# A recurrent step of 36 single-column products: joint gate banks, an earlier cell tanh, `h2` by halves and a new order of products

## What is computed

```python
xi = xt @ U_i + b_i;  xg = xt @ U_c + b_c;  xo = xt @ U_o + b_o     # all steps
def step(h, c):
    i = sigmoid(xi_t + h @ V_i)
    g = tanh(xg_t + h @ V_c)
    o = sigmoid(xo_t + h @ V_o)
    c_new = h * c + i * g          # the factor of c is h; the f gate is not used
    h_new = o * tanh(c_new)
```

## Time and profile before

| | us |
|---|---|
| Median of 3 runs | 21443.61 (21435.93 to 21449.04) |
| The profiled execution, its own time | 21427.66 |
| Its span (first to last instruction) | 21425.9 |
| TensorE, products busy | 14188.0 (66%) |
| TensorE, weight loads busy (beside the products) | 10794.4 (50%) |
| VectorE busy | 11134.5 (52%) |
| ScalarE busy | 7413.2 (35%) |
| GpSimd busy | 6033.6 (28%) |

### The profile page before, as it was taken

The page is one execution under the profiler, slowest core; times in us unless marked ns, Lnnn a source line. Parts: engine busy times, 40 slices in busy tenths (PEclk is TensorE's granted clock), DMA queues, the critical chain, the costliest instruction groups (busy, mean ns, idle before and its releaser), DMA issues. The chain is left out here.

```text
span 21425.9 us, 696512 instructions
## 1 busy us (share of the span) xinstructions
PE 14188.0 (66%) x249848; PEld 10794.4 (50%) x249849; DVE 11134.5 (52%) x57848; ACT 7413.2 (35%) x56381; POOL 6033.6 (28%) x6537
## 2 busy tenths in 40 slices
PE   5416778822883565665777777777777777777776
PEld 3211236621452444444566666666666666666665
DVE  6325666641125545445455555555555555555555
ACT  0007841100110020010255555555555555555554
POOL 1676666675705747657100000000000000000000
PEclk9858987756996777777755555555555555555555
DMA  0000012301003333333100000000000000000000
GB/s 29 16 5 5 1 39 82 81 12 48 23 25 98 103 75 102 89 88 102 32 4 4 4 4 4 4 4 4 4 4 4 4 4 4 4 4 4 4 4 15
DMA packets 344107, 610.30 MB, mean 28 GB/s; under 512 B 152419, under 2 KB 222154, under 8 KB 340328
## 3 DMA queue, kind: packets, MB, share of 16 engines
q0 software_dynamic: 251520, 473.04, 8.8%
q1 hardware_dynamic: 89704, 98.43, 1.4%
HBM read 506.71 MB, written 64.29 MB: 27 GB/s over the span
## 5 line engine op out<-in xcount | busy, mean ns | idle before, releaser
L2024 PE MATMUL lr_Z<-ls_h,ls_V 128*128 128x1 f16 x225000 | 7182.9, 166 | 2968.8 <-DVE ls_h L2072 2828.3
L2024 PEld LDWEIGHTS lr_Z<-ls_h,ls_V 128*128 128x128 f16 x225000 | 6670.4, 105 | 3969.6 <-DVE ls_h L2072 3825.8
L2066 DVE SCALAR_TENSOR_TENSOR ls_c<-ls_S,ls_hc 128x1 f32<-128x1 f32 x12500 | 2371.0, 219 | 3616.6 <-ACT ls_S L2042 3616.6
L2041 ACT ACTIVATE ls_S<-lr_Z 128x1 f32<-128x1 f32 x12500 | 2068.8, 171 | 5248.9 <-PE lr_Z L2024 5248.9
L1985 POOL COPY ls_HT<-ls_h 128x250 f32 x50 | 19.8, 395 | 10760.5 <-DVE ls_h L2074 10760.5
L620 PE MATMUL prop_sum<-prop_G,prop_S 128*128 128x256 f32 x5040 | 1903.9, 557 | 1668.5 <-DMA prop_G<-hop_table,prop_idx 1267.3
L607 POOL DMA_INDIRECT prop_G<-hop_table,prop_idx x2520 | 2388.0, 948 | 1353.1 <-issue 807.2
L620 PEld LDWEIGHTS prop_sum<-prop_G,prop_S 128*128 128x128 f32 x5040 | 1432.1, 292 | 2140.2 <-issue 955.0
L2072 DVE TENSOR_TENSOR ls_h<-ls_S,ls_th 128x1 f16<-128x1 f32 x12500 | 1892.1, 162 | 800.6 <-ACT ls_th L2049 9.9
L2049 ACT ACTIVATE ls_th<-ls_c 128x1 f32<-128x1 f32 x12500 | 2095.6, 198 | 0.0
L2046 ACT ACTIVATE ls_S<-lr_Z 128x1 f32<-128x1 f32 x12500 | 2068.7, 171 | 0.0
(11 more groups left out here) (407 smaller groups left out, 14492.9 us busy)
## 6 DMA issues: line engine op xcount, KB each, us to landing
prop_G<-hop_table,prop_idx POOLq DMA_INDIRECT x2520
hop_table<-gnn_H SPq DMA_DIRECT2D x3, 6400.0 KB, 20.3
me_W<-in_L_ffn_W SPq DMA_DIRECT2D x16, 1024.0 KB, 10.8
moe_out<-me_Ys SPq DMA_DIRECT2D x108, 128.0 KB, 1.7
gm_AG<-gat_atable,gm_idx POOLq DMA_INDIRECT x840
gs_G<-gat_table,gs_idx POOLq DMA_INDIRECT x840
sd_records<-sc_ring_recsd,sc_ring_placesd POOLq DMA_INDIRECT x784, 2.1
ss_records<-me_ring_recss,me_ring_placess POOLq DMA_INDIRECT x432, 2.1
```

The source lines that it names most:

```text
L2024: mm = nc.tensor.matmul(Z[hf][bank][:, col:col + 1], (V2 if part == "21" else V1)[:, q, ROWS.index(row), :], hx[:, prev, q:q + 1], start=F ...
L2041: nc.scalar.activation(S[:, s % 2, m:m + 1], Z[hf][m][:, col:col + 1], ACT.Sigmoid, scale=back)
L2066: nc.vector.scalar_tensor_tensor(c[:, e, m:m + 1], S[:, e, KD + m:KD + m + 1], S[:, e, m:m + 1], hc[:, m:m + 1], ALU.mult, ALU.add).then_i ...
```

## The change

1. `PLACE` puts i0 and i1 into bank 0, g0 alone into bank 1, g1 alone into bank 2, and o0 and o1 into bank 3.
2. `ORDER` is a list written out product by product. The first 18 finish g0 (at the 15th) and i0 and i1 (at the 18th), products 19 to 24 finish g1, and 25 to 36 both output rows. The first product that reads the second half of `h1` is the fifth; the first to read `h2` of the first half is the twelfth, of the second half the fifteenth.
3. TensorE waits once per step for each of the four semaphores (`h1_made[0]`, `h1_made[1]`, `h2_made[0]`, `h2_made[1]`), in front of the first product that needs it.
4. ScalarE has six instructions a step: tanh of g0, sigmoid of both i, tanh of g1, tanh of the first half of the cell, sigmoid of both o, tanh of the second half of the cell. Each has its own wait.
5. VectorE computes `h2` in two halves directly from its sources, h2 = tanh(c) * o - h1 (with o as a per-partition scalar operand), behind both halves of `h1`; `h` and `hc` come after it. The first cell update waits for g0 and both i, the second for g1; the first half of `h1` waits for the output gates, the second for the second tanh.
6. `h1` and `h2` keep two steps rather than 250.

```diff
-PLACE = {"i0": (0, 0), "g0": (0, 1), "i1": (1, 0), "g1": (1, 1), "o0": (2, 0), "o1": (3, 0)}
+PLACE = {"i0": (0, 0), "i1": (0, 1), "g0": (1, 0), "g1": (2, 0), "o0": (3, 0), "o1": (3, 1)}
...
-ORDER = (terms("i0 g0 i1 g1", "11 21", 0) + terms("i0 g0 i1", "11 21", 1)
-         + [t for q in range(KD) for t in terms("i0 g0", "12", q)]
-         + terms("g1", "11 21", 1) + [t for q in range(KD) for t in terms("i1 g1", "12", q)]
-         + [t for row in ("o0", "o1") for q in range(KD) for t in terms(row, "11 21 12", q)])
+ORDER = terms("g0.21.0 i0.21.0 i1.11.0 i0.11.0 i1.11.1 i0.21.1 g0.11.0 i0.11.1 g0.21.1 g0.11.1 i1.21.0 "
+              "i0.12.0 i1.12.0 g0.12.0 g0.12.1 i0.12.1 i1.21.1 i1.12.1 "
+              "g1.11.0 g1.12.0 g1.11.1 g1.21.1 g1.12.1 g1.21.0 "
+              "o1.21.1 o1.11.1 o0.21.0 o0.11.0 o1.11.0 o0.12.0 o0.12.1 o1.12.1 o0.21.1 o1.21.0 o1.12.0 o0.11.1")
...
-        h1 = ph.sb("h1", [P, BODY, KD], F16)
-        h2 = ph.sb("h2", [P, BODY, KD], F16)
+        h1 = ph.sb("h1", [P, 2, KD], F16)
+        h2 = ph.sb("h2", [P, 2, KD], F16)
...
-                                hx, made = (h2, h2_made) if part == "12" else (h1, h1_made[q])
-                                if (part == "12", q) not in waited:
-
+                                hx, made = (h2, h2_made[q]) if part == "12" else (h1, h1_made[q])
+                                if made not in waited:
                                     pe.wait_ge(made, i * BODY + s + 1)
                                     waited.append(made)
...
-                            for m in range(KD):
-                                act.wait_ge(z[m], t + 1)
-                                nc.scalar.activation(S[:, s % 2, m:m + 1], Z[hf][m][:, col:col + 1], ACT.Sigmoid, scale=back)
-                                nc.scalar.activation(S[:, s % 2, KD + m:KD + m + 1], Z[hf][m][:, col + 1:col + 2], ACT.Tanh,
-                                                     scale=back).then_inc(gates[m], 1)
-                            for m in range(KD):
-                                act.wait_ge(z[2 + m], t + 1)
-                                nc.scalar.activation(S[:, s % 2, 2 * KD + m:2 * KD + m + 1], Z[hf][2 + m][:, col:col + 1], ACT.Sigmoid, scale=back)
-                            for m in range(KD):
-                                act.wait_ge(cell[m], t + 1)
-                                nc.scalar.activation(th[:, s % 2, m:m + 1], c[:, s % 2, m:m + 1], ACT.Tanh).then_inc(tanh_made[m], 1)
+                            act.wait_ge(z[1], t + 1)
+                            nc.scalar.activation(S[:, e, KD:KD + 1], Z[hf][1][:, col:col + 1], ACT.Tanh, scale=back)
+                            act.wait_ge(z[0], t + 1)
+                            nc.scalar.activation(S[:, e, 0:KD], Z[hf][0][:, col:col + KD], ACT.Sigmoid, scale=back).then_inc(i_made, 1)
+                            act.wait_ge(z[2], t + 1)
+                            nc.scalar.activation(S[:, e, KD + 1:KD + 2], Z[hf][2][:, col:col + 1], ACT.Tanh, scale=back).then_inc(g_made, 1)
+                            act.wait_ge(cell[0], t + 1)
+                            nc.scalar.activation(th[:, e, 0:1], c[:, e, 0:1], ACT.Tanh)
+                            act.wait_ge(z[3], t + 1)
+                            nc.scalar.activation(S[:, e, 2 * KD:M6], Z[hf][3][:, col:col + KD], ACT.Sigmoid, scale=back).then_inc(o_made, 1)
+                            act.wait_ge(cell[1], t + 1)
+                            nc.scalar.activation(th[:, e, 1:2], c[:, e, 1:2], ACT.Tanh).then_inc(th1_made, 1)
...
-                                dve.wait_ge(tanh_made[m], t + 1)
-                                nc.vector.tensor_tensor(h1[:, s, m:m + 1], S[:, e, 2 * KD + m:2 * KD + m + 1], th[:, e, m:m + 1],
+                                dve.wait_ge(o_made if m == 0 else th1_made, t + 1)
+                                nc.vector.tensor_tensor(h1[:, e, m:m + 1], S[:, e, 2 * KD + m:2 * KD + m + 1], th[:, e, m:m + 1],
                                                         ALU.mult).then_inc(h1_made[m], 1)
+                            for m in range(KD):
+                                dve.wait_ge(h1_made[m], t + 2)
+                                nc.vector.scalar_tensor_tensor(h2[:, e, m:m + 1], th[:, e, m:m + 1], S[:, e, 2 * KD + m:2 * KD + m + 1],
+                                                               h1[:, e, m:m + 1], ALU.mult, ALU.subtract).then_inc(h2_made[m], 1)
                             nc.vector.tensor_tensor(h[:, s, :], S[:, e, 2 * KD:M6], th[:, e, :], ALU.mult).then_inc(h_made, 1)
                             dve.wait_ge(h_made, t + 1)
-                            nc.vector.tensor_tensor(h2[:, s, :], h[:, s, :], h1[:, s, :], ALU.subtract).then_inc(h2_made, 1)
                             nc.vector.tensor_tensor(hc[:], h[:, s, :], c[:, e, :], ALU.mult).then_inc(hc_made, 1)
```

More of the change, by code:

```diff
@@ L1812, with terms @@
 ROWS = [g + str(m) for g in GATES for m in range(KD)]
-PLACE = {"i0": (0, 0), "g0": (0, 1), "i1": (1, 0), "g1": (1, 1), "o0": (2, 0), "o1": (3, 0)}
+PLACE = {"i0": (0, 0), "i1": (0, 1), "g0": (1, 0), "g1": (2, 0), "o0": (3, 0), "o1": (3, 1)}
 BANKS = 4
-def terms(rows, parts, q):
-    return [(row, part, q) for row in rows.split() for part in parts.split()]
-ORDER = (terms("i0 g0 i1 g1", "11 21", 0) + terms("i0 g0 i1", "11 21", 1)
-         + [t for q in range(KD) for t in terms("i0 g0", "12", q)]
-         + terms("g1", "11 21", 1) + [t for q in range(KD) for t in terms("i1 g1", "12", q)]
-         + [t for row in ("o0", "o1") for q in range(KD) for t in terms(row, "11 21 12", q)])
+def terms(text):
+    return [(row, part, int(q)) for row, part, q in (t.split(".") for t in text.split())]
+ORDER = terms("g0.21.0 i0.21.0 i1.11.0 i0.11.0 i1.11.1 i0.21.1 g0.11.0 i0.11.1 g0.21.1 g0.11.1 i1.21.0 "
+              "i0.12.0 i1.12.0 g0.12.0 g0.12.1 i0.12.1 i1.21.1 i1.12.1 "
+              "g1.11.0 g1.12.0 g1.11.1 g1.21.1 g1.12.1 g1.21.0 "
+              "o1.21.1 o1.11.1 o0.21.0 o0.11.0 o1.11.0 o0.12.0 o0.12.1 o1.12.1 o0.21.1 o1.21.0 o1.12.0 o0.11.1")
 assert len(ORDER) == len(set(ORDER)) == 3 * KD * M6
@@ L1975, in lstm_layer @@
             z = [pr.sem(f"z{g}") for g in range(BANKS)]
-            gates, cell, tanh_made, h1_made = ([pr.sem(f"{n}{j}") for j in range(KD)] for n in ("gates", "cell", "tanh", "h1_"))
-            h_made, h2_made, hc_made, kept = (pr.sem(n) for n in ("h", "h2", "hc", "kept"))
+            cell, h1_made, h2_made = ([pr.sem(f"{n}{j}") for j in range(KD)] for n in ("cell", "h1_", "h2_"))
+            i_made, g_made, o_made, th1_made, h_made, hc_made, kept = (pr.sem(n) for n in ("i", "g", "o", "th1", "h", "hc", "kept"))
             with pr.block() as block:
@@ L2012, in _ @@
                         for s in range(BODY):
-                            hf, prev = s // HALF, (s - 1) % BODY
+                            hf, prev = s // HALF, (s - 1) % 2
                             waited = []
@@ L2054, in _ @@
                     for m in range(KD):
-                        nc.vector.memset(h1[:, BODY - 1, m:m + 1], 0.0).then_inc(h1_made[m], 1)
-                    nc.vector.memset(h2[:, BODY - 1, :], 0.0).then_inc(h2_made, 1)
+                        nc.vector.memset(h1[:, 1, m:m + 1], 0.0).then_inc(h1_made[m], 1)
+                        nc.vector.memset(h2[:, 1, m:m + 1], 0.0).then_inc(h2_made[m], 1)
                     nc.vector.memset(hc[:], 0.0).then_inc(hc_made, 1)
@@ L2061, in _ @@
                             for m in range(KD):
-                                dve.wait_ge(gates[m], t + 1)
                                 if m == 0:
                                     dve.wait_ge(hc_made, t + 1)
-                                nc.vector.scalar_tensor_tensor(c[:, e, m:m + 1], S[:, e, KD + m:KD + m + 1], S[:, e, m:m + 1], hc[:, m:m + 1],
-                                                               ALU.mult, ALU.add).then_inc(cell[m], 1)
+                                    dve.wait_ge(i_made, t + 1)
+                                else:
+                                    dve.wait_ge(g_made, t + 1)
+                                nc.vector.scalar_tensor_tensor(c[:, e, m:m + 1], S[:, e, KD + m:KD + m + 1], S[:, e, m:m + 1],
+                                                               hc[:, m:m + 1], ALU.mult, ALU.add).then_inc(cell[m], 1)
                             if s % HALF == 0:
```

2 lines of the change are left out of this document (1 added, 1 removed).

## The result

| | before | after |
|---|---|---|
| Median, us | 21444.75 (4 runs) | 21701.06 (4 runs, 21695.46 to 21705.34) |
| The profiled execution, its own time | 21427.66 | 21703.19 |
| Ratio after/before, 95% interval | | 1.012 (1.0102 to 1.0137) |
| Length of most steps, us | 1.700 | 1.733 |
| Steps over 0.2 us longer than that, turns left out | 0 | 200 |

The changed kernel is 256 us slower. The forecast was 21250, faster. The step was to be 1.669 us and is 1.733; and there is a second loss, steps that are 0.23 or 0.34 longer than the others, of which the forecast knew nothing. A turn is the jump from one body of 250 steps to the next.)

A forecast was written before the change was run, and what follows sets the result against it. The prediction took latency round the ring of one recurrent step, 1.700 us, as the bound. Its terms summed to 1.669 a step, 6250 x 0.031 = 194 us saved, giving 21250 us; the range for 8 in 10 was 21040 to 21445.

The forecast's parts named there:

- gate to cell: From the joint input sigmoid's start to the first cell update: 0.205 us instead of 0.266, saving 0.061 a step.
- Products: TensorE's 36 products a step: count and pace of 0.027 us stay, so fewer waits bring zero.
- rival 4: TensorE's pace moves with the waits gone, or the clock goes to 2.4 GHz: about 1.44 a step, 19,800 us; chance 0.02.
- The wait at product 15: TensorE's fifteenth load waits for the second half of `h2`: 0.009 us a step.
- Tanh to `h1`: First cell tanh to first `h1`, output sigmoid now behind the tanh: gap 0.101, sigmoid 0.167, in all 0.301 instead of 0.226.
- Rival 1: On ScalarE the output sigmoid goes 0.067 behind the first cell tanh: step 1.636, 400 us less, 21044; chance 0.12.
- Rival 3: On ScalarE the output sigmoid waits for the whole first tanh, 0.203: step 1.771, 444 us more, 21888; chance 0.09.
- `h2` per half: On VectorE the second half of `h2` starts 0.135 us behind the first, making the fifteenth product 0.009 late.
- Rival 2: On VectorE the halves of `h2` are 0.16 apart, the second 0.037 late: step 1.697, 19 us less, 21425; chance 0.12.
- `h` and `hc`: On VectorE, moved behind both halves of `h2`: `hc` ends 0.59 after the load, hidden with 0.30 to spare.
- The sum: Whole step: 1.669 us against 1.700; 6250 x 0.031 = 194 us saved, forecast median 21250.
- The second half of `h1`: Comes 0.093 us behind the first half, the second tanh waiting for the output sigmoid; hidden with 0.019 to spare.

The follow-up runs named there:

- Experiments 1 and 2: First: changed kernel, gates' wait put before the `hc` wait, 21268.98 us, ratio 0.9921; second: kernel before, `hc` wait put before the gates' wait, 21723.11 us, ratio 1.0132.
- experiment 1: Changed kernel with the wait for the input gates put before the wait for `hc` at the first cell update; 21268.98 us, ratio 0.9921 to before.
- experiment 5, e10: e1_swap with VectorE's semaphores raised by one before the loop and all its waits at t + 2; 22927.01 us on a slower chip, ratio 0.9908 to before.
- experiment 6: Five edits to e1_swap, each alone: output sigmoid first, `h2` in one instruction behind `h`, single sigmoids, old product order, wait every load; steps 1.686, 1.721, 1.714, 1.784, 1.667.
- experiment 6, fifth: e1_swap with a wait in front of every one of the 36 weight loads, as before; step 1.667, 23044 us against 23141 for before.
- e1_swap: Changed kernel with the gates' wait before the `hc` wait at the first cell update; 21268.98 us, ratio 0.9921 to before, step 1.667.
- e12: e10 run again on the chip of e11; 21213.21 us against 21420.23 for before, ratio 0.9904.
- e11: e1_swap run again, on one chip with e12; 21255.17 us against 21420.23 for before, ratio 0.9922.
- e2: Kernel before with the `hc` wait moved ahead of the gates' wait at the first cell update; 21723.11 us, ratio 1.0132 to before.
- e5: Changed kernel with a third wait, for `hc` once more, behind the two at the first cell update; step 1.720, 23379 us against 23141 for before.

## Why the prediction was wrong, point by point

**The step that failed: gate to cell.** "Now i is last, one instruction ..., so 0.172 + 0.033 = 0.205" took the 0.033 from a wait that the update carries itself. It does in the kernel before, where the gates' wait stands first. The diff puts it second, and the update then carries the wait for `hc`: 0.274. That is 0.069 too little there, against 0.005 too much in the other parts together: 0.064 a step, 400 us of the 469 between the forecast of the profiled run, 21234, and that run. Experiments 1 and 2 show it from both sides. The row was there to be read: the trace of before has a semaphore instruction on L2064 in every step and none on L2062. I had listed the added waits, but asked of none which instruction carries it and what is behind it. The rivals didn't have it either: the slower one put the loss on ScalarE, between tanh and sigmoid, where there was none.

**What was missing: the long steps.** 57 us of the 469; 10 more come from ahead of the recurrence. They fall on the edges of the blocks of 128. That an edge costs something where VectorE's stream isn't issued ahead is an inference, from where the eight places are and what removed them: it isn't issued ahead where a wait stands outside of an instruction and is met late (in front of the cell update) or where the value of the waits is replaced (in front of `h2`). Each of the two has its four places in a body, and each went with its own edit: the first four with experiment 1, the others with experiment 5 or 6. The forecast said of the turns alone that issue takes time, and the sum had no term for it elsewhere.

**Right, or nearly:**
- *Products.* Zero for the waits: experiment 6, fifth. The pace is 0.0267 a load and the clock half, as before: rival 4 is out. The wait at product 15 was to be 0.009 and is about 0.012 (its load goes 0.388 after the first, the pace alone gives 0.376); first load to sigmoid 0.696 against 0.692.
- *Tanh to `h1`.* The gap behind the tanh is 0.109, I took 0.101; the sigmoid behind it takes 0.153, I took 0.167; in sum 0.295 against 0.301. Rival 1, a gap of 0.067, is out. The figure of the Trainium skill (ScalarE: Activation LUTs, "What ACT_TABLE_LOAD costs", an overlap of about 93 ns) gave 0.110 for the gap; the trace agrees, 0.203 - 0.109 = 0.094. Rival 3, beside which the prediction named the Trainium skill's rule (Advanced Engine Details and Errata, "The Read-Write Bubble"), isn't seen: by their rows the two overlap by those 0.094.
- *`h2` per half.* The two are 0.136 apart, from 4.008 to 4.144 in the changed kernel; taken 0.135. Rival 2 is out.
- *`h` and `hc`.* `hc` ends at 4.62, 0.60 after the load; taken 0.59. Hidden.
- *The sum.* With the waits in the other order it holds: 1.669 was said, 1.667 is measured; 21250 was said, 21269 and 21255 are measured. The 19 us between forecast and e1_swap are 35 of long steps, which the sum didn't have, less 12 for the shorter step.
- *The second half of `h1`.* 0.091 behind the first half in the changed kernel, taken 0.093. In e1_swap, whose step I had meant, it is 0.101, since the second tanh waits for its cell: the near tie fell the other way, and product 5 still doesn't wait (its load goes at 0.110, the pace alone gives 0.109).

**What stays open.** What VectorE's issue side does in the 0.036 before the semaphore instruction and the 0.045 behind it. Why the third wait saves 0.013. Why the step of e12 is 1.663 where e10's, the same kernel, is 1.667: the fifth load goes at 0.105 rather than 0.109, but in e11 it goes at 0.106 and the step is 1.667. What happens at a block's edge: the packets of the blocks are in the trace, the reason for the delay isn't.

## What to carry to other kernels

Where an instruction has more than one wait, put first the one that is met last: the instruction carries the first, the others are carried out on the issue side, and there a wait that is met last cost 0.055 to 0.07 us more here, in every step, and four long steps a body went with it. Read in the trace of which line the semaphore instructions are, before and after an edit; it is a row like any other. Keep the waits of a step at one value if they read a register: here the second value was set only when the waits with the first were met, and taking it out removed the other four long steps.

## What the runs showed of the hardware

- VectorE starts 0.033 after the end of a ScalarE instruction whose semaphore it carries itself, and 0.09 to 0.10 after it where the wait is an instruction of its own (after, e2, e5 against before, e1). The Trainium skill describes the two ways (Advanced Engine Details and Errata, "Sequencer Loop": an engine instruction goes into a queue and waits there for its semaphores, a control instruction is executed by the sequencer). The trace agrees, and gives the price.
- VectorE's instructions come in blocks of 128, in packets of 8,192 bytes: a grid of 14.2 steps at 9 instructions a step, 12.8 at 10, 11.6 at 11. An edge cost 0.23 or 0.34 us in eight places of a body of the changed kernel, and nothing in any place of the kernel before. The Trainium skill has 256 instructions to a line of the instruction cache (Advanced Engine Details and Errata, "ISA Cache"). The trace agrees for TensorE, whose packets have 16,384 bytes and come every 3.47 steps at 73.8 instructions a step; for VectorE and ScalarE it has half of that, and the measurement decides.
- A register that holds the value of open waits is rewritten only after the last of them has been met: 0.014 to 0.016 after the start of the last instruction that carries one, which is the second half of `h1` in the changed kernel, `h2` in the kernel before and `hc` in e10_one_value.
- ScalarE: a sigmoid of two columns from PSUM takes 0.172 from idle and 0.153 right behind a tanh that reads SBUF; instructions follow such a short one at 0.05, not 0.067.
